# Selective scan in a hybrid block: projection and causal convolution as two products each, in place of one folded set of taps

## The reference

```python
x_res = x @ W_x.T
z = x @ W_z.T
params = x @ W_params.T                      # 64 + 16 + 16 columns
dt = softplus(params[..., :R] @ W_dt.T + b_dt)
conv = conv_general_dilated(x_res, conv_w, padding=[(K - 1, 0)], feature_group_count=d)   # K = 4
u = silu(conv)
A = -exp(A_log)                              # 256 channels x 16 states
A_tilde = exp(dt[..., None] * A)
B_tilde = where(abs(A) < 1e-8, dt[..., None], (A_tilde - 1) / (A + 1e-10))
h = A_t * h + B_t * Bp_t[:, None, :] * u_t[:, :, None]    # over the tokens
y_t = einsum('bn,bdn->bd', Cp_t, h)
y = (y + u * D_param) * silu(z)
out = y @ W_out.T
```

## Time and profile before

| | |
|---|---|
| median of 3 runs | 2104.65 us (2103.42 to 2106.32) |
| the profiled execution's own time | 2105.05 us |
| its span in the profile | 2103.3 us |
| busy, share of the span: PE, DVE, ACT, POOL | 92%, 80%, 51%, 36% |
| scan's block | from 1264.6 us to about 1850 us |
| pieces of PE in the span | 6834 |

### The profile page before, as it was taken

How to read it: one execution, slowest core, us unless ns; L and a number is a source line. 1 busy time by engine, 2 the same in 40 slices (tenths; PEclk the granted TensorE clock), 3 DMA queues, 4 the chain that set the end, 5 groups by cost and what they waited for, 6 DMA issues and landing times. The chain is left out here.

```text
span 2103.3 us, 25351 instructions
## 1 busy us (share of the span) xinstructions
PE 1938.0 (92%) x6834; PEld 728.0 (35%) x6834; DVE 1676.9 (80%) x2442; ACT 1062.5 (51%) x1399; POOL 755.2 (36%) x517
## 2 busy tenths in 40 slices
PE   8997999999999999999999997788888988799997
PEld 4441332322232323322444443233333333244443
DVE  5889998998998988964565578999999999945554
ACT  3541666665666666672222236576557557422221
POOL 4662110000000000000100029999999999810000
PEclk9996999999999999999999998999999989999998
DMA  3652112321211121213100013444444445300000
GB/s 103 142 128 52 41 42 45 66 45 42 42 47 42 41 47 41 41 50 118 40 0 0 0 62 92 125 114 118 117 115 116 117 117 152 88 0 20 20 10 31
DMA packets 94539, 138.23 MB, mean 66 GB/s; under 512 B 13600, under 2 KB 52656, under 8 KB 92880
## 3 DMA queue, kind: packets, MB, share of 16 engines
q1 hardware_dynamic: 94416, 136.73, 26.1%
HBM read 110.21 MB, written 26.08 MB: 65 GB/s over the span
## 5 line engine op out<-in xcount | busy, mean ns | idle before, releaser
L915 DVE TENSOR_REDUCE mx<-max_bank 128x1 f32<-128x512 f32 x960 | 617.9, 686 | 64.6 <-PE max_bank L824 64.3
L901 ACT ACTIVATE probs<-score_bank 128x1024 f32<-128x1024 f32 x512 | 496.9, 1021 | 289.2 <-PE score_bank L838 289.0
L824 PE MATMUL max_bank<-ks,qs 96*128 96x512 bf16 x960 | 335.6, 390 | 0.0
L838 PE MATMUL score_bank<-qs,ks 99*128 99x512 bf16 x1024 | 313.2, 389 | 14.9 <-issue 10.2
L1700 POOL TENSOR_TENSOR ring<-u,bc 128x1024 f32<-128x1024 f32 x128 | 302.6, 2374 | 0.0
L1770 PE MATMUL ys_bank<-outs,rec_diag 128*128 128x512 f32 x512 | 253.9, 626 | 45.6 <-POOL outs L1708 23.0
L884 PE MATMUL o_bank<-probs,vg 128*32 128x512 f32 x2048 | 275.4, 610 | 0.7 <-ACT probs L901 0.7
L1708 POOL TENSOR_TENSOR outs<-ring,bc 128x1024 f32<-128x1024 f32 x109 | 258.7, 2373 | 26.3 <-DVE ring L2079 26.3
L784 POOL CAST neg_parts<-neg_max 16x128 bf16<-16x128 f32 x31 | 8.8, 282 | 656.9 <-DVE neg_max L928 656.9
L1935 ACT ACTIVATE a_bank<-dt,decay_s 128x512 f32<-128x512 f32 x256 | 169.4, 684 | 147.4 <-DVE ring L2079 105.6
L1451 ACT ACTIVATE relu_f<-hid_bank_f 128x512 f32<-128x512 f32 x128 | 76.5, 597 | 327.3 <-PE hid_bank_f L1376 282.3
(11 more groups left out here) (216 smaller groups left out, 2149.4 us busy)
## 6 DMA issues: line engine op xcount, KB each, us to landing
bc<-bc_scr SPq DMA_DIRECT2D x128, 512.0 KB, 4.9
qk_parts<-parts SPq DMA_DIRECT2D x128, 96.0 KB, 1.9
qs<-qk_parts SPq DMA_DIRECT2D x128, 64.0 KB, 4.1
o_scr<-o_sb SPq DMA_DIRECT2D x32, 256.0 KB, 2.1
ks<-qk_parts SPq DMA_DIRECT2D x16, 384.0 KB, 4.7
xin<-in_x_dram SPq DMA_DIRECT2D x8, 512.0 KB, 3.9
ks<-qk_parts SPq DMA_DIRECT2D x16, 256.0 KB, 3.5
qs<-qk_parts SPq DMA_DIRECT2D x32, 128.0 KB, 4.7
```

The lines of the kernel that those rows point to most:

```text
L824: nc.tensor.matmul(max_bank[(r + a) % MB][:], qs[r][0:SROWS, half, j, qt * P:(qt + 1) * P], ks[r][0:SROWS, j, kh * TW:(kh + 1) * TW], star ...
L838: mm = nc.tensor.matmul(score_bank[pair][:, j % 2], ks[r][0:MROWS, j, kt * P:(kt + 1) * P], qs[r][0:MROWS, qh, j, :], start=True, stop=True)
L901: nc.scalar.activation(probs[:, s % 2, 2 * pair:2 * pair + 2], score_bank[pair][:], ACT.Exp, scale=SOFTMAX_SCALE).then_inc(probs_ready, 1)
L915: nc.vector.tensor_reduce(mx[:, a // HU, a % HU:a % HU + 1], max_bank[(r + a) % MB][:], AX_X, ALU.max)\
```

## The change

The projection and the convolution are done apart. `x_res`, a buffer of 2 x 1027 columns (one batch and three zeros ahead of it), keeps W_x's result; `tap_diag` holds eight diagonal matrices, ident times conv_w of a tap and chunk. For each chunk PE makes the residual (2 products, `residual`), ACT copies it into x_res (`keep_residual`), and PE makes the four taps as products of a diagonal with shifted columns of x_res (`u_taps`): 4 + 8 products a tile in place of 16. In the scan the residual of chunk 0 is made at n = 4 and kept at n = 5, that of chunk 1 made at n = 6 and kept at n = 7; the taps of chunk 0 follow at n = 8, those of chunk 1 at n = 10, and SiLU of chunk 0 moves from n = 7 to n = 9, behind the exponentials. At the end of the feed-forward the residuals stand around the step sizes, and the copies ahead of each chunk's absolute value.

DVE builds the eight diagonals (128 x 128) where it had made four folded weights (128 x 512). Two broadcast loads of conv_w become one small one. In the scan the softplus's e_part, relu_part and log_part share the buffers of the norm (xc, sq, and log_var with guess_rs); dt is in two buffers, the first made with the first tile. The last feed-forward's weights, loaded in the last tile, go to x_res's space in place of wtap's.

```diff
@@ feed_forward
+            def residual(f):
+                for c in range(DC):
+                    mm = nc.tensor.matmul(u_banks[f][:], w["wx"][:, c, f * P:(f + 1) * P],
+                                          xn_scan[:, c, TAPS - 1:TAPS - 1 + TW], start=(c == 0), stop=(c == DC - 1))
+                mm.then_inc(res_made, 1)
+
+            def keep_residual(act, f):
+                act.wait_ge(res_made, f + 1)
+                nc.scalar.activation(w["x_res"][:, f, TAPS - 1:TAPS - 1 + TW], u_banks[f][:], ACT.Copy).then_inc(res_kept, 1)
...
             if begun is not None:
+                residual(0)
                 pe.wait_ge(par_kept, 1)
...
-                pe.wait_ge(taps_set, TAPS + DC)
+                residual(1)
+                pe.wait_ge(taps_set, TAPS * DC + DC)
                 for f in range(DC):
+                    pe.wait_ge(res_kept, f + 1)
                     for tap in range(TAPS):
-                        for c in range(DC):
-                            mm = nc.tensor.matmul(u_banks[f][:], w["wtap"][:, tap, c, f * P:(f + 1) * P],
-                                                  xn_scan[:, c, tap:tap + TW],
-                                                  start=(tap == 0 and c == 0), stop=(tap == TAPS - 1 and c == DC - 1))
+                        mm = nc.tensor.matmul(u_banks[f][:], w["tap_diag"][:, tap * DC + f], w["x_res"][:, f, tap:tap + TW],
+                                              start=(tap == 0), stop=(tap == TAPS - 1))
...
                 for f in range(DC):
+                    keep_residual(act, f)
                     act.wait_ge(dt_made, f + 1)
...
-                        nc.vector.tensor_tensor(w["wtap"][:, tap], w["wtap"][:, tap], w["wx"][:], ALU.mult).then_inc(taps_set, 1)
+                        for c in range(DC):
+                            nc.vector.tensor_scalar(w["tap_diag"][:, tap * DC + c], w["ident"][:], w["conv"][:, c, tap:tap + 1], None,
+                                                    ALU.mult).then_inc(taps_set, 1)
@@ scan_weights
-    loads += [(w["wtap"][:, :, c, :], io["conv"].partition_broadcast(P)) for c in range(DC)]
@@ scan
-        e_part, relu_part, log_part = (m.sb(n, [P, DC, TW]) for n in ("e_part", "relu_part", "log_part"))
+        xc, sq, logs = (m.sb(n, [P, DC, TW]) for n in ("xc_s", "sq_s", "logs"))
+        e_part, relu_part, log_part, log_var, guess_rs = xc, sq, logs, logs[:, 0], logs[:, 1]
...
+            def residual(t, f, bank):
+                product(bank, [(wx[:, c, f * P:(f + 1) * P], xn[:, c, at(t)]) for c in range(DC)], res_made)
+
+            def u_taps(t, f, bank):
+                pe.wait_ge(res_kept, DC * t + f + 1)
+                product(bank, [(tap_diag[:, tap * DC + f], x_res[:, f, at(t, TAPS - 1 - tap)]) for tap in range(TAPS)], u_made)
...
-                            u_taps(t + 1, 0, (0, 1), w1[:])
+                            residual(t + 1, 0, w1[:])
                         if n == 5:
 
                             pe.wait_ge(par_kept, t + 2)
                             step_size(t + 1, 0, w0[:])
-                            u_taps(t + 1, 0, (2,), w1[:])
                         if n == 6:
-                            u_taps(t + 1, 0, (3,), w1[:])
+
+                            pe.wait_ge(res_kept, DC * (t + 1) + 1)
+                            residual(t + 1, 1, w1[:])
...
                         if n == 8:
 
+                            pe.wait_ge(res_kept, DC * (t + 1) + DC)
+                            u_taps(t + 1, 0, w1[:])
+                        if n == 10:
+
                             pe.wait_ge(u_kept, DC * (t + 1) + 1)
-                            u_taps(t + 1, 1, (0, 1), w1[:])
-                        if n == 9:
-                            u_taps(t + 1, 1, (2, 3), w1[:])
...
+            def keep_residual(t, f, bank):
+                act.wait_ge(res_made, DC * t + f + 1)
+
+                act.wait_ge(u_made, DC * t)
+                nc.scalar.activation(x_res[:, f, at(t)], bank, ACT.Copy).then_inc(res_kept, 1)
...
+                        if n == 5:
+                            keep_residual(t + 1, 0, w1[:])
                         if n == 6:
                             soft_split(t + 1, 0, w0[:])
                         if n == 7:
-                            silu_u(t + 1, 0, w1[:])
-                            exp_tables()
+                            keep_residual(t + 1, 1, w1[:])
                         if n == 8:
                             soft_split(t + 1, 1, w0[:])
                         if n == 9:
                             soft_exp(t + 1, 0)
                             soft_exp(t + 1, 1)
+                            silu_u(t + 1, 0, w1[:])
+                            exp_tables()
```

More of the change, by code:

```diff
@@ L1322, in _ @@
             if begun is not None:
-                nc.gpsimd.memset(xn_scan[:, :, 0:TAPS - 1], 0.0).then_inc(consts_set, 1)
+                nc.gpsimd.memset(w["x_res"][:, :, 0:TAPS - 1], 0.0).then_inc(consts_set, 1)
                 nc.gpsimd.memset(begun["ones"][:], 1.0).then_inc(consts_set, 1)
@@ L1579, in scan_weights @@
         ("wx", [P, DC, D]), ("wz", [P, DC, D]), ("wout", [P, DC, D]), ("wpar", [P, DC, R + 2 * NS]), ("wdt", [R, D]),
-        ("wtap", [P, TAPS, DC, D]), ("b_dt", [P, DC]), ("d_par", [P, DC]), ("ident", [P, P]), ("decay", [P, 6, DC, NS]))}
+        ("tap_diag", [P, TAPS * DC, P]), ("conv", [P, DC, TAPS]), ("x_res", [P, DC, TAPS - 1 + S]), ("b_dt", [P, DC]), ("d_par", [P, DC]), ("ident", [P, P]), ("decay", [P, 6, DC, NS]))}
     loads = [(to, io[n].rearrange("(c p) n -> p c n", p=P)) for to, n in
@@ L1605, in scan @@
         m = Mem(nc, ctx)
-        wz, wout, wtap, wpar, wdt, b_dt = (w[n] for n in ("wz", "wout", "wtap", "wpar", "wdt", "b_dt"))
+        wx, wz, wout, tap_diag, x_res, wpar, wdt, b_dt = (w[n] for n in (
+            "wx", "wz", "wout", "tap_diag", "x_res", "wpar", "wdt", "b_dt"))
         a_col, is_small = w["decay"][:, 1], w["decay"][:, 2]
-        d_diag, rec_diag, ones, small_int, par, dt, bc = (begun[n] for n in (
-            "d_diag", "rec_diag", "ones", "small_int", "par", "dt", "bc"))
+        d_diag, rec_diag, ones, small_int, par, bc = (begun[n] for n in (
+            "d_diag", "rec_diag", "ones", "small_int", "par", "bc"))
+        dt = [begun["dt0"], m.sb("dt1", [P, DC, TW])]
         u = [begun["u0"], m.sb("u1", [P, DC, TW])]
@@ L1743, in parameters @@
                 product(w0[0:R + 2 * NS], [(wpar[:, c], xn[:, c, at(t)]) for c in range(DC)], par_made)
-            def u_taps(t, f, taps, bank):
-                for tap in taps:
-                    for c in range(DC):
-                        mm = nc.tensor.matmul(bank, wtap[:, tap, c, f * P:(f + 1) * P], xn[:, c, at(t, TAPS - 1 - tap)],
-                                              start=(tap == 0 and c == 0), stop=(tap == TAPS - 1 and c == DC - 1))
-                if taps[-1] == TAPS - 1:
-                    mm.then_inc(u_made, 1)
+            def residual(t, f, bank):
[3 more added lines that the diff above has]
+                product(bank, [(tap_diag[:, tap * DC + f], x_res[:, f, at(t, TAPS - 1 - tap)]) for tap in range(TAPS)], u_made)
             def step_size(t, f, bank):
@@ L1868, in guess @@
                     act.wait_ge(stepped, 3 * k)
-                nc.scalar.activation(log_var[:], w0[:], ACT.Ln, bias=eps_col[:]).then_inc(guessed, 1)
+                nc.scalar.activation(log_var, w0[:], ACT.Ln, bias=eps_col[:]).then_inc(guessed, 1)
                 act.wait_ge(guessed, 2 * k + 1)
-                nc.scalar.activation(guess_rs[:], log_var[:], ACT.Exp, scale=-0.5).then_inc(guessed, 1)
+                nc.scalar.activation(guess_rs, log_var, ACT.Exp, scale=-0.5).then_inc(guessed, 1)
             def keep_par(t):
@@ L1934, in make_decay @@
                                 act.wait_ge(state_kept, states_before(g - 2) + 1)
-                    nc.scalar.activation(a_bank[g % 2][:, f], dt[:, t % 2, f], ACT.Exp, scale=a_col[:, f, n:n + 1])\
+                    nc.scalar.activation(a_bank[g % 2][:, f], dt[t % 2][:, f], ACT.Exp, scale=a_col[:, f, n:n + 1])\
                         .then_inc(decays, 1)
@@ L2038, in soft @@
                     dve.wait_ge(decays, DC * NS * (t - 1))
[L2039 removed]
+                nc.vector.tensor_tensor(dt[t % 2][:, f], bank, relu_part[:, f], ALU.add).then_inc(soft_made, 1)
             def gate(t):
```

35 lines of the change are left out of this document (16 added, 19 removed).

## The result

The changed kernel takes 2111.44 us (median of 15 runs, 2106.15 to 2114.05). The kernel before, run beside it 15 times, takes 2105.3. The ratio is 1.0028, with a 95% interval of 1.002 to 1.0036: slower by 5.9 us, which is over the 0.2% that can be told from no change. The forecast was 2109.9, in a range of 2103 to 2117, slower at 0.74. The profiled execution took 2112.11 us, its span is 2110.3.

A forecast was written before the change was run, and what follows sets the result against it. The prediction took DVE's own work plus its waits for ACT's late decays as the bound. Tiles +6.7 us and start -1.5 summed to +5.2, giving a profile of 2110.3 and a median of 2109.9 us; range 2103 to 2117.

The forecast's parts named there:

- The bound: In the scan, DVE's own work plus its waits for ACT's late decays, 21.3 us inside the tiles, sets the pace.
- D(8): Moment DVE starts the scale of state 8, chunk 0, in a scan tile; no longer late, -8.2 us in sum.
- States 9 to 12: ACT's queue in the scan runs without a gap; D(12) 2.24 us later after D(8) in even tiles, 1.97 in odd.
- D(10): Moment DVE starts the scale of state 10, chunk 0, in a scan tile; forecast 0.5 to 0.7 us late.
- D(11): Moment DVE starts the scale of state 11, chunk 0, in a scan tile; forecast 1.7 to 2.0 us late.
- D(12): Moment DVE starts the scale of state 12, chunk 0, in a scan tile; forecast 1.7 to 2.0 us late.
- PE's products: Four fewer products in each of seven prepared tiles, 24 us of PE time in the scan, costed at nothing.
- The start: First tile's preparation at the feed-forward's end; the wait for taps gives way to one for the softplus, -1.5 us.
- The copies and small edits: ACT's x_res copies, DVE's diagonals, loads and shared buffers; all at nothing, diagonals some 2 us at most without PE's cover.
- A: Rival: POOL sets the scan's pace, so no change; only the start counts, 2103.2 us; chance 0.10.
- C: Rival: at PE's lower clock, taps reach SiLU 1 us late in each tile, 7 us more, 2117 us; chance 0.11.
- B: Rival: faster, D(8) stops being late and the moved SiLU falls into ACT's free time; 2095 us; chance 0.07.

The follow-up runs named there:

- e8: e6 with, at the feed-forward's end, both residuals made after the step sizes and their copies put behind ACT's exponentials; 2083.93 us, ratio 0.9893.
- e1: The kernel before with only chunk 0's SiLU moved from behind state 7 to behind state 9's exponentials, chunk 1's taps following at state 10; 2119.34 us.
- e3: The changed kernel with the two products of each residual made twice in the scan, 16 products a tile again; 2119.46 us, ratio 1.0063.
- e2: The changed kernel with the next tile's preparation drawn one state forward, SiLU of chunk 0 at state 8; 2100.36 us, ratio 0.9975.
- e7: The kernel before, folded taps kept, with its SiLUs and PE steps put in e6's order; 2097.23 us, ratio 0.9957.
- e6: e2 with chunk 0's taps ahead of state 6's sum and the second SiLU moved to state 12, ahead of the second "one"; 2087.21 us.
- e5: The changed kernel with ACT making each x_res copy of a tile twice, first into a spare buffer; 2113.1 us, ratio 1.0031.
- e4: The changed kernel with POOL weighing only chunk 0 of states 8 to 11 from the second tile on; 2111.76 us, ratio 1.0029.

## Why the prediction was right, and where it was not

**The bound.** Right. In every kernel the time follows DVE's waits for ACT in the tiles, to which the start's -0.9 (e8: -2.3) is added where the copies are in. Against the kernel before, waits and start make +5.3 us for the change and its median is 6.1 longer; e1 +11.6 and +13.7, e3 +12.3 and +13.9, e2 -4.3 and -5.2, e7 -9.9 and -8.0, e6 -18.7 and -18.0, e8 -20.4 and -21.3. The 2 us by which e1 and e7 miss are in the traces, at the scan's end, where PE makes its last sums; e1, then the kernel before:

```profile
1852.49 5.82 PE L1770 MATMUL ys_bank<-outs,rec_diag 128*128 128x512 f32 x8 [0.70 <-POOL outs L1708]
```

```profile
1839.94 3.78 PE L1770 MATMUL ys_bank<-outs,rec_diag 128*128 128x512 f32 x8 [1.56 <-POOL outs L1708]
```

Over the 10 us around these rows the granted clock is 0.66 in e1 and 1.00 in the kernel before. From DVE's last scale to the end of the span it is 265.9 us in the kernel before and in the changed one, and 267.9 to 268.0 in e1, e5, e6 and e7. With this term no kernel misses by more than 1.5 us, which stays open.

**D(8).** -8.2 was forecast and came: no D(8) is late. But SiLU's place, the reason given, was not all of it. One row of the waits of the kernel before was not read:

```profile
ACT u L1886 <- PE work L1748: 2.4, 3, 1.2
```

In tiles 3, 5 and 6 SiLU itself waited for the taps, and by these 2.4 us D(8) was later there than in the other tiles of their kind (1.55 and 0.85 against 0.61, 2.21 against 0.99). The first eight pieces of the taps took 5.40, 4.70 and 5.78 us in these three tiles and 3.60 to 3.81 in the other four (granted clock 0.64 in tile 6, 1.00 in tile 4). So PE's products were on the path in the kernel before as well. Moving SiLU is enough to cure D(8): in e1 and e3 no D(8) is late either, though the products are back.

**States 9 to 12.** Right in place and nearly in size. Forecast 0.5 to 0.7 for D(10), 1.7 to 2.0 for D(11) and D(12); measured 0.70, 1.86, 1.69 in even tiles and 0.42, 1.61, 1.48 in odd ones. D(12) comes 18.25 us after D(8) in tile 4 (1592.05 to 1610.30), which is the forecast's figure. The sum in the tiles was forecast at +6.7 and is +6.2. SiLU behind state 9 does not wait for its taps: in tile 4 they end at 1595.97 (1592.37 and 3.60), and it starts at 1597.04.

**PE's products.** The step that was wrong: "I cost it at nothing", since all of it lay beside DVE's 69 us a tile against PE's 62. PE is indeed less busy, from 481.38 us in the scan to 464.71, 17 and not 24, and the granted clock over the scan fell from 0.92 to 0.90: part of the products took longer. But the removed products were worth 5 to 7 us of DVE's waits here (5.4 by e1, 7.0 by e3), in time 8 us in both runs, e1's with the start and the scan's end in it. Most of it falls in tiles in which PE ran at its lower clock, 4.9 of 5.4 us in e1 and 4.6 of 7.0 in e3.

That the sum came out right all the same is in part luck. It took ACT's queue to be held by nothing but ACT's own work, which holds for the changed kernel only because the products are gone: with them, D(9) and D(10) are later, and the forecast neither saw that loss nor priced its cure. A forecast for the move alone by the same steps would have missed by 8 us, as the expectation for e1 did. The share of a tile that PE is busy was read where its order ahead of ACT had to be. The rows to read were ACT's waits for PE: that for SiLU's taps, which was there, and that for the second step size, which SiLU hid in the kernel before.

**The start.** Forecast -1.5, measured -0.9. The wait for taps gave way to one for the softplus, as forecast. ACT's last ReLU ended at 1255.2, 0.3 later than the chain of the forecast put it (1253.6, and 1.3 for this execution's late arrival), and DVE's softplus took 4.7 us instead of 4.35, mostly by the wait of 0.46 between two of its own steps.

**The copies and small edits.** At nothing, and e5 shows it for the copies. The shared buffers, loads and diagonals were not tried apart; in all kernels with them the tiles' time is accounted for by the waits above.

**The rivals.** A falls by e4. C was right as a mechanism and wrong in place: in tiles 3 and 4 the first residual runs wholly or in part at the lower clock (four pieces in 3.62 us at 1503.73, in 2.85 at 1577.77), but SiLU's new place leaves time for it. In e2 there is none, and it costs up to 1.69 us in a tile. The lower clock is also in the kernel before, where it made D(8) later by 2.4 us in all, and in e1, e3 and e7. B, that SiLU falls into ACT's free time, was wrong for state 9, but 0.07 said too little of what lies beside it: one state earlier that free time is there, and e2 and e6 have it.

## What to carry to other kernels

An engine's free time is a place, not a sum: a block with two table loads costs some 1.8 us a tile more one state later, where another such block follows (tile 4: DVE waits 2.48 us in e2 and 4.25 in the changed kernel). Where several blocks are put by hand into an in-order queue, write down for each deadline how far the queue is ahead there, and place the blocks so that each gap takes one. And before pricing removed work at nothing, look at who will wait for it in the new order: the thing that hid it may be what the same change moves away.

## What the runs showed of the hardware

- Two products of 512 columns, four pieces in the rows, take 1.88 to 1.99 us at the full clock and 3.78 at a granted clock of 0.50 (e2, e3), each time behind 1.2 to 1.5 us of waiting. A wait alone does not say it, as e2's tile 4 shows.
- The same instructions meet the lower clock in one kernel and not in another. The last eight pieces of the scan's sums take 3.78 us in the kernel before and the changed one and 5.75 to 5.85 in e1, e5, e6 and e7, which makes these four 2 us longer. Which tile meets it changes from kernel to kernel as well: in tile 4, chunk 0's first product takes 1.99 us in e2, 2.85 in the changed kernel and 3.78 in e3.
- A dependent step on DVE waits 0.46 us for the one before it in the second chunk of the first softplus (1262.79, and 1260.73 in e8); in the first chunk no wait is shown.
- Beside POOL's long product in the block ahead of the scan, one DVE instruction takes 3.78 us, over five times as long as the others of its line. From the changed kernel, timelines of POOL and DVE, then the groups of DVE from 1245 to 1254:

```profile
1246.59 7.03 POOL L1348 TENSOR_TENSOR rec_diag<-ident_s,decay_s 128x4096 f32<-128x4096 f32 x1
```

```profile
1245.61 4.87 DVE L1558 SCALAR_TENSOR_TENSOR count_f<-y_bank_f,count_f 128x512 f32<-128x512 f32 x8
...
1250.39 4.38 DVE L1566 SCALAR_TENSOR_TENSOR xT<-count_f,xT 128x512 f32<-128x512 f32 x2
```

```profile
L1566 DVE SCALAR_TENSOR_TENSOR xT<-count_f,xT 128x512 f32<-128x512 f32 x1 | 3.8, 3775 | 0.0
```

The pair of L1566 is one instruction of 3.78 us, which ends at 1254.16, 0.54 behind POOL's product, and one of 0.68 behind it. The 14 others of this line in this feed-forward, without such a product beside them, take 0.68. L1566 reads both inputs from SBUF. L1558, of the same kind but with one input from a PSUM bank, takes 0.68 beside POOL's product too. The Trainium skill ("GPSIMD Engine Reference", Key points) says that GpSimd shares its SBUF interfaces with VectorE, with contention for DVE instructions of two SBUF inputs; the rows agree in kind, and no run was made for it. The 3.78 us lie ahead of the softplus in every kernel here, in that of before too.
